# A loop over batches written out on all five engines of a fused attention and mixture-of-experts kernel

## Chip, core and metric

The kernel runs on one core of a Trainium2 chip. The metric is the device time of one launch in microseconds; lower is better. A core has five engines with an instruction stream each: TensorE (PE in the profile; its weight loads are PEld), VectorE (DVE), ScalarE (ACT), GpSimd (POOL) and SyncE (SP). They meet only at semaphores, and a transfer signals its end by a semaphore too. PEq, DVEq and so on in a row stand for the engine's sequencer, which reads the instructions, works out register values and takes the branches.

## What is computed

`x` is 4 batches x 1024 tokens x 256 features, `ctx` is 4 x 154 x 256. All data is float32.

```
x = x + softmax((LN(x) Wq + bq)(ctx Wk + bk)^T / 16, masked) (ctx Wv + bv)
t = LN(x)
scores = sigmoid(l2norm(t) l2norm(gate_w)^T)          # 16 experts
combine = the 8 largest scores of a token, divided by their sum, else 0
routed = sum over e of combine[e] * ((silu(t w_gate[e]) * (t w_up[e])) w_down[e])
shared = (silu(t sw_gate) * (t sw_up)) sw_down
x = x + routed + shared
```

## The kernel before

**Tiling.** The 4096 tokens are 8 chunks of 512 tokens, two chunks (`hf` 0 and 1) to a batch `b`. All 17 experts (the shared one is expert 0) are applied to every token; each expert's weights stay in SBUF, split into a high and a low part, so that every product is three matmuls (`three_pass`, L298 to L300). For one chunk and one expert PE does `gate_up`: twelve matmuls of 512 columns into `gate_ps` and `up_ps`, and `down`: twelve of 256 columns into `y_ps`. Between them ACT takes the tanh (`tanh_gate`, L666), DVE multiplies by gate and up (`silu_up`, L949 and L953), POOL multiplies by the combine weight (`weighted`, L1160), ACT copies out the high part (`hidden_hi`, L673) and DVE the low part (`hidden_lo`, L959). The hidden values have two buffers. `gate_up` runs three experts ahead of `down`.

**Order of work.** Each engine has a function `chunk(b, hf, ahead, last)` with one step for each of the 17 experts. In between the steps stand the parts of the *front* of the next chunk: layer norm, attention, second layer norm, router, put at steps written out by hand (`PE_AT`, `ACT_AT`, `DVE_AT`, `POOL_AT`). So PE's stream in a chunk is a fixed sequence: `down` 0, `gate_up` 3, `down` 1, `gate_up` 4 and so on, with the front's transposes (L386) and small matmuls between. The first transposes of the front (`turn_x`) come at step 2.5.

**Combine weights.** ACT stores the combine rows to memory (L659), and SP loads them again, two experts at a time, broadcast to all 128 partitions (`spread`, L256, 512 KB each written in SBUF) into four places `cb`. The first four of a chunk are issued together near the end of the chunk before. SP also loads the next `xin` (x rows) and stores the finished chunk (L272).

**The loop.** Before the loop each engine runs a prologue: keys, values, weight loads and splits, and the whole front of chunk 0. Then the chunks 0 to 5 stand in a hardware loop of three passes, one on each engine (SP L281, PE L555, ACT L750, DVE L1077, POOL L1191); chunks 6 and 7 are written out behind it:

```python
with pe.Fori(0, B - 1) as b:
    chunk(b, 0, True, False)
    chunk(b, 1, True, False)
chunk(B - 1, 0, True, False)
chunk(B - 1, 1, False, True)
```

Inside it `b` is a register, so every wait count that `upto` gives is worked out by the sequencer. `wait_apart` is used where such a count stands with other waits: it puts the counts in registers, waits for `consts_set` (long set), and then for the semaphores. A pass holds two chunks. A loop's branch stands on the loop's line in the profile; it is taken twice and falls through once.

Of the kernel before, what the change touches and what calls it, by code (L numbers as in the profile page):

```python
# [50 lines left out]
def xattn_moe_kernel(nc, x, ctx, mask, Wq, bq, Wk, bk, Wv, bv, gate_w, w_gate, w_up, w_down,  # L51
                     sw_gate, sw_up, sw_down, out):
    B, S, D = x.shape
    KEYS = ctx.shape[1]
    E, _, H = w_gate.shape
    TOK = 512
    TILES = TOK // P
# [21 lines left out]
    with ExitStack() as stack:  # L79
# [107 lines left out]
            return b * (2 * per) + (per * hf + k)  # L187

        def first_chunk(b, hf):
            return isinstance(b, int) and b == 0 and hf == 0  # L190

        def wait_apart(eng, *waits):


            counts = [n if isinstance(n, int) else eng.to_reg(n) for _, n in waits]
            eng.wait_ge(consts_set, 1)
            for (what, _), n in zip(waits, counts):
                eng.wait_ge(what, n)

        def due(table, step, at):  # L200
# [15 lines left out]
        def _(sp):  # L216
# [30 lines left out]
            def spread(b, hf, pair):  # L247

                stored_c = (c_stored, upto(b, hf, 16, 16))
                if pair >= PLACES:  # L250
                    wait_apart(sp, (h_done, upto(b, hf, NE, 2 * (pair - PLACES) + 3 + FREE)))
                elif first_chunk(b, hf):
                    wait_apart(sp, stored_c)
                else:
                    wait_apart(sp, (h_done, upto(b, hf - 1, NE, 2 * (pair + PLACES) + 3 + FREE)), stored_c)
                sp.dma_start(cb[:, pair % PLACES].rearrange("p a t -> p (a t)"),  # L256
                             c_rows[2 * pair:2 * pair + 2, :].rearrange("a t -> (a t)").partition_broadcast(P)) \
                    .then_inc(cb_loaded[pair % PLACES], 16)
# [4 lines left out]
            def chunk(b, hf, load):  # L263
                for pair in range(PLACES, PAIRS):
                    spread(b, hf, pair)
                if load:
                    sp.wait_ge(x2_made, upto(b, hf, 2, 4))
                    sp.dma_start(xin[:], x_rows[b * 2 + (hf + 2)]).then_inc(x_loaded, 16)
                for pair in range(PLACES):
                    spread(b, hf + 1, pair)  # L270
                sp.wait_ge(y_added, upto(b, hf, 2, 2 + FREE))
                sp.dma_start(out_rows[b * 2 + hf], x2[:, hf]).then_inc(stored, 16)  # L272
# [5 lines left out]
                    sp.dma_start(out_rows[CHUNKS - 1, :, 2 * q:2 * q + 2, :], x2[:, 1, 2 * q:2 * q + 2, :]) \  # L278
                        .then_inc(stored, 16)

            with sp.Fori(0, B - 1) as b:  # L281
                chunk(b, 0, True)
                chunk(b, 1, True)
            chunk(B - 1, 0, False)
# [7 lines left out]
        def _(pe):  # L292
# [96 lines left out]
            def turn_x(b, hf, k):  # L389
                if k == 0 and not first_chunk(b, hf):  # L390
                    pe.wait_ge(c_read, upto(b, hf, 1, 0))
                turn_ln(ln1_done, t1_turned, b, hf, k)
# [66 lines left out]
            def gate_up(b, hf, e):  # L459
                hf, e = nxt(hf, e)  # L460
                i, par = slot(hf, e), hf % 2
                if e == 0:
                    pe.wait_ge(t2_hi, upto(b, hf, 2, 2))
                    pe.wait_ge(t2_lo, upto(b, hf, 2, 2))
                if hf == 0:
                    pe.wait_ge(w_hi, e + 1)
                    pe.wait_ge(w_lo, e + 1)
                for ps, col, free, done in ((gate_ps, 0, silu_done, gate_done), (up_ps, UP0, prod_done, up_done)):
                    pe.wait_ge(free, upto(b, hf, NE, e - 1 + FREE))
                    ins = three_pass(ps[i][:], [((W[:, e, HI, col + k * H:col + (k + 1) * H],  # L470
                                                  W[:, e, LO, col + k * H:col + (k + 1) * H]),
                                                 (xT[:, par, HI, k, :], xT[:, par, LO, k, :])) for k in range(KD)],
                                     first=True, last=True)
                    ins.then_inc(done, 1)
# [38 lines left out]
            def chunk(b, hf, ahead, last):  # L513
                for s in range(NE):
                    down(b, hf, s)
                    if ahead:
                        front(s, b, hf + 1)
                    if s + 3 < NE or not last:
                        gate_up(b, hf, s + 3)
                    if ahead:  # L520
                        front(s + .5, b, hf + 1)
# [30 lines left out]
            turn_c(0, 0)  # L552
            gate_up(0, 0, 1)
            gate_up(0, 0, 2)
            with pe.Fori(0, B - 1) as b:  # L555
                chunk(b, 0, True, False)
                chunk(b, 1, True, False)
            chunk(B - 1, 0, True, False)
# [4 lines left out]
        def _(act):  # L563
# [47 lines left out]
            def split_w(e):  # L611
                act.wait_ge(staged[e % STAGES], 48 * (e // STAGES + 1))
                af(W[:, e, HI, :], stage[:, e % STAGES, :], ACT.Copy).then_inc(w_hi, 1)
# [36 lines left out]
            def combine_rows(b, hf):  # L650
                act.wait_ge(c_turned, upto(b, hf, 1, 1))
                if not first_chunk(b, hf):
                    act.wait_ge(c_stored, upto(b, hf, 16, 0))
                af(cT[0:E, :], f_ps[1][0:E, :], ACT.Copy).then_inc(c_read, 1)
                act.wait_ge(c_read, upto(b, hf, 1, 1))
                if not first_chunk(b, hf):
                    for done in cb_loaded:
                        act.wait_ge(done, upto(b, hf, 32, 0))
                act.dma_start(c_rows, cT[0:E, :]).then_inc(c_stored, 16)  # L659
# [32 lines left out]
            def chunk(b, hf, ahead, last):  # L692
                for s in range(NE):
                    if s + 2 < NE or not last:
                        tanh_gate(b, hf, s + 2)
                    if ahead:
                        front(s, b, hf + 1)
                    if s + 1 < NE or not last:
                        hidden_hi(b, hf, s + 1)
                    if ahead:  # L700
                        front(s + .5, b, hf + 1)
# [45 lines left out]
            hidden_hi(0, 0, 0)  # L747
            for e in SPLITS["end"]:
                split_w(e)
            with act.Fori(0, B - 1) as b:  # L750
                chunk(b, 0, True, False)
                chunk(b, 1, True, False)
            chunk(B - 1, 0, True, False)
# [4 lines left out]
        def _(dve):  # L758
# [57 lines left out]
            def split_w(e):  # L816
                dve.wait_ge(w_hi, e + 1)
                V_.tensor_tensor(W[:, e, LO, :], stage[:, e % STAGES, :], W[:, e, HI, :].bitcast(F32),
                                 ALU.subtract).then_inc(w_lo, 1)
# [184 lines left out]
            def chunk(b, hf, ahead, last):  # L1004
                for s in range(NE):
                    if s + 2 < NE or not last:
                        silu_up(b, hf, s + 2)
                    if ahead:
                        front(s, b, hf + 1)
                    if s + 1 < NE or not last:  # L1010
                        hidden_lo(b, hf, s + 1)
                    if ahead:
                        front(s + .5, b, hf + 1)
                add_y(b, hf)
# [59 lines left out]
            hidden_lo(0, 0, 0)  # L1074
            for e in SPLITS["end"]:
                split_w(e)
            with dve.Fori(0, B - 1) as b:  # L1077
                chunk(b, 0, True, False)
                chunk(b, 1, True, False)
            chunk(B - 1, 0, True, False)  # L1080
# [4 lines left out]
        def _(pool):  # L1085
# [61 lines left out]
            def weighted(b, hf, e):  # L1147
                hf, e = nxt(hf, e)
                i = slot(hf, e)
                if e == 0:  # L1150
                    wait_apart(pool, (prod_done, upto(b, hf, NE, 1 + FREE)), (h_hi, upto(b, hf, NE, FREE - 1)),
                               (h_lo, upto(b, hf, NE, FREE - 1)))
                    pg.tensor_scalar(h[:, i, :], ew[:, i, :], 0.5, 1.0, ALU.mult, ALU.mult).then_inc(h_done, 1)
                else:
                    pool.wait_ge(prod_done, upto(b, hf, NE, e + 1 + FREE))
                    pool.wait_ge(h_hi, upto(b, hf, NE, e - 1 + FREE))
                    pool.wait_ge(h_lo, upto(b, hf, NE, e - 1 + FREE))
                    pair = (e - 1) // 2
                    pool.wait_ge(cb_loaded[pair % PLACES], upto(b, hf, 32, 16 * (pair // PLACES + 1)))
                    pg.tensor_tensor(h[:, i, :], ew[:, i, :], cb[:, pair % PLACES, (e - 1) % 2, :], ALU.mult) \  # L1160
                        .then_inc(h_done, 1)
# [12 lines left out]
            def chunk(b, hf, ahead, last):  # L1174
                for s in range(NE):
                    if s + 1 < NE or not last:
                        weighted(b, hf, s + 1)
                    if ahead:
                        front(s + .5, b, hf + 1)
# [8 lines left out]
            ln2_std(0, 0)  # L1188
            inverse_norm(0, 0)
            weighted(0, 0, 0)  # L1190
            with pool.Fori(0, B - 1) as b:  # L1191
                chunk(b, 0, True, False)
                chunk(b, 1, True, False)
            chunk(B - 1, 0, True, False)
# [24 lines left out]
```

## Time and profile before

| | us |
|---|---|
| median of 3 runs | 715.76 |
| the runs | 711.46, 715.76, 718.47 |
| span of the profiled execution | 717.8 |
| PE busy in the span | 691.6 (96%) |
| PE weight loads busy | 595.8 (83%) |
| DVE busy | 459.2 (64%) |
| POOL busy | 260.7 (36%) |
| ACT busy | 239.8 (33%) |
| mean granted TensorE clock | 0.981 |

The profiled execution has no separately listed time beside its span of 717.8 us; that is the number the sums are made against. Busy time of PE is that of matmuls whose ends are modelled and which overlap, so 96% says that they followed one another closely, not that the array was used to its peak. A granted clock of 1.00 is 2.4 GHz, 0.50 is 1.2 GHz.

### The profile page before, as it was taken

The numbers are of one execution on the slowest core, as the hardware profiler recorded it, in microseconds if no ns is written. First come the engines' busy times: TensorE is split into PE (matmuls) and PEld (weight loads), VectorE is DVE, ScalarE is ACT, GpSimd is POOL, SyncE is SP. The second block draws the span as 40 slices with busy tenths as digits, with TensorE's granted clock in tenths as the row PEclk, the third lists the DMA queues.
The fourth block names the chain that finished last, engine by engine and source line by source line (L and its number), as shares of the span: only waits on it lengthen the run. The fifth ranks groups of instructions, "written<-read, shape, count | busy, mean of one in ns | idle before, by whom it ended". The sixth has DMA issues, their size and how long they took to land.

```text
span 717.8 us, 11775 instructions
## 1 busy us (share of the span) xinstructions
PE 691.6 (96%) x3995; PEld 595.8 (83%) x3995; DVE 459.2 (64%) x1029; ACT 239.8 (33%) x485; POOL 260.7 (36%) x222
## 2 busy tenths in 40 slices
PE   7997799999999899999999899999999999999997
PEld 6575688888888788888888788888988888888886
DVE  4576666677667475777566576677565775775444
ACT  4345233333424134233333234242334233232221
POOL 2120432535343242435344243434324343433432
PEclk9799999999999899999999999999999999999999
DMA  6315511032110510005100411005110421006100
GB/s 184 111 32 162 184 60 46 13 103 106 59 31 1 180 60 30 30 24 185 59 30 1 151 59 60 30 2 192 46 58 0 136 94 38 1 3 204 61 0 31
DMA packets 32772, 51.30 MB, mean 71 GB/s; under 512 B 3918, under 2 KB 24391, under 8 KB 32711
## 3 DMA queue, kind: packets, MB, share of 16 engines
q1 hardware_dynamic: 32455, 50.23, 21.6%
q8 instruction: 37, 0.61, 0.4%
q10 hardware_dynamic: 256, 0.26, 0.2%
q14 instruction: 24, 0.20, 0.1%
HBM read 46.03 MB, written 4.46 MB: 70 GB/s over the span
## 4 chain that ended last, share of the span: by engine, by line
PE 91%; issue 4%; DVE 2%; POOL 1%; ACT 1%; DMA 1%; POOLq 0%; SPq 0%; DVEq 0%; ACTq 0%
PE y_ps L298 9%; PE y_ps L300 9%; PE y_ps L299 9%; PE gate_ps L298 9%; PE up_ps L298 9%; PE gate_ps L300 9%; PE gate_ps L299 8%; PE up_ps L300 8%; PE up_ps L299 8%; PE f_ps L386 2%; PE f_ps L408 2%; PE f_ps L419 1%; PE up_ps L368 1%; PE up_ps L307 1%; DMA xin<-in_x_dram 1%
## 5 line engine op out<-in xcount | busy, mean ns | idle before, releaser
L1160 POOL TENSOR_TENSOR hidden<-hidden,cb 128x512 f32<-128x512 f32 x128 | 200.1, 1565 | 308.2 <-DVE hidden L953 257.4
L949 DVE SCALAR_TENSOR_TENSOR hidden<-hidden,gate_ps 128x512 f32<-128x512 f32 x136 | 93.2, 685 | 156.2 <-ACT hidden L666 145.9
L666 ACT ACTIVATE hidden<-gate_ps 128x512 f32<-128x512 f32 x136 | 81.5, 599 | 275.0 <-PE gate_ps L300 273.4
L298 PE MATMUL y_ps<-W,hs 128*128 128x256 f32 x544 | 157.9, 290 | 13.4 <-issue 5.7
L300 PE MATMUL y_ps<-W,hs 128*128 128x256 f32 x544 | 154.8, 284 | 0.0
L299 PE MATMUL y_ps<-W,hs 128*128 128x256 f32 x544 | 154.5, 284 | 0.0
L298 PEld LDWEIGHTS y_ps<-W,hs 128*128 128x128 f32 x544 | 103.8, 191 | 19.9 <-issue 9.5
L959 DVE TENSOR_TENSOR hs<-hidden,hs 128x512 fp32r<-128x512 f32 x136 | 95.6, 703 | 29.1 <-ACT hs L673 29.1
L298 PE MATMUL gate_ps<-xT,W 128*128 128x512 f32 x272 | 109.1, 401 | 0.0
L298 PE MATMUL up_ps<-xT,W 128*128 128x512 f32 x272 | 108.8, 400 | 0.0
L300 PE MATMUL gate_ps<-xT,W 128*128 128x512 f32 x272 | 108.2, 398 | 0.0
L299 PE MATMUL gate_ps<-xT,W 128*128 128x512 f32 x272 | 107.8, 396 | 0.0
L299 PE MATMUL up_ps<-xT,W 128*128 128x512 f32 x272 | 107.6, 396 | 0.0
L300 PE MATMUL up_ps<-xT,W 128*128 128x512 f32 x272 | 107.5, 395 | 0.0
L299 PEld LDWEIGHTS y_ps<-W,hs 128*128 128x128 f32 x544 | 103.9, 191 | 3.9
L953 DVE TENSOR_TENSOR hidden<-hidden,up_ps 128x512 f32<-128x512 f32 x136 | 93.6, 688 | 16.6 <-PE up_ps L300 1.9
L300 PEld LDWEIGHTS y_ps<-W,hs 128*128 128x128 f32 x544 | 103.9, 191 | 0.0
L673 ACT ACTIVATE hs<-hidden 128x512 fp32r<-128x512 f32 x136 | 85.2, 626 | 47.2 <-POOL hidden L1160 47.2
L300 PEld LDWEIGHTS up_ps<-xT,W 128*128 128x128 f32 x272 | 51.6, 190 | 12.8
L299 PEld LDWEIGHTS up_ps<-xT,W 128*128 128x128 f32 x272 | 52.0, 191 | 12.0
L298 PEld LDWEIGHTS up_ps<-xT,W 128*128 128x128 f32 x272 | 51.5, 189 | 12.1
L300 PEld LDWEIGHTS gate_ps<-xT,W 128*128 128x128 f32 x272 | 51.7, 190 | 11.6
(141 smaller groups left out, 726.3 us busy)
## 6 DMA issues: line engine op xcount, KB each, us to landing
cb<-c_rows SPq DMA_DIRECT2D x64, 512.0 KB, 4.2
xin<-in_x_dram SPq DMA_DIRECT2D x8, 512.0 KB, 3.8
out_dram<-x SPq DMA_DIRECT2D x7, 512.0 KB, 7.4
stage<-in_L_ffn_w_gate_dram SPq DMA_DIRECT2D x16, 128.0 KB, 2.3
stage<-in_L_ffn_w_up_dram SPq DMA_DIRECT2D x16, 128.0 KB, 2.5
stage<-in_L_ffn_w_down_dram SPq DMA_DIRECT2D x16, 128.0 KB, 2.6
cb<-in_ctx_dram SPq DMA_DIRECT2D x1, 512.0 KB
out_dram<-x SPq DMA_DIRECT2D x2, 256.0 KB, 2.1
```

Source lines behind the costliest of these rows:

```text
L298: mm(ps, lh, rh, start=first and i == 0, stop=False)
L299: mm(ps, lh, rl, start=False, stop=False)
L300: ins = mm(ps, ll, rh, start=False, stop=last and i == len(pairs) - 1)
L307: nc.tensor.transpose(up_ps[0][:, 0:P], ident[:], ident[:])
L386: ins = nc.tensor.transpose(f_ps[k][:, j * P:(j + 1) * P], xn[:, j, k * P:(k + 1) * P], ident[:])
L408: mm(to[:, 0:2 * KEYS], xT[:, par, HI, k, c], A[:, bi, k].rearrange("p s q -> p (s q)"), start=k == 0, stop=False)
L666: af(ew[:, i, :], gate_ps[i][:], ACT.Tanh, scale=0.5).then_inc(tanh_done, 1)
L673: af(hs[:, i, HI, :], h[:, i, :], ACT.Copy).then_inc(h_hi, 1)
L949: V_.scalar_tensor_tensor(out=ew[:, i, :], in0=ew[:, i, :], scalar=1.0, in1=gate_ps[i][:], op0=ALU.add, op1=ALU.mult).then_inc(silu_done, 1)
L953: V_.tensor_tensor(ew[:, i, :], ew[:, i, :], up_ps[i][:], ALU.mult).then_inc(prod_done, 1)
L959: V_.tensor_tensor(hs[:, i, LO, :], h[:, i, :], hs[:, i, HI, :].bitcast(F32), ALU.subtract) \
L1160: pg.tensor_tensor(h[:, i, :], ew[:, i, :], cb[:, pair % PLACES, (e - 1) % 2, :], ALU.mult) \
```

## The change

The five loops become Python loops, so that the program holds the body three times on each engine, with `b` a number: every wait count is a constant, and there is no loop register and no branch in the stream. `first_chunk` and `wait_apart` lose the parts that dealt with registers; `wait_apart` no longer waits for `consts_set`. Which engine does what, in which order, with which buffers and semaphores otherwise stays as it was.

```diff
         def first_chunk(b, hf):
-            return isinstance(b, int) and b == 0 and hf == 0
+            return b == 0 and hf == 0
 
         def wait_apart(eng, *waits):
-            counts = [n if isinstance(n, int) else eng.to_reg(n) for _, n in waits]
-            eng.wait_ge(consts_set, 1)
-            for (what, _), n in zip(waits, counts):
+            for what, n in waits:
                 eng.wait_ge(what, n)
...
-            with sp.Fori(0, B - 1) as b:
+            for b in range(B - 1):
                 chunk(b, 0, True)
                 chunk(b, 1, True)
             chunk(B - 1, 0, False)
...
-            with pe.Fori(0, B - 1) as b:
+            for b in range(B - 1):
                 chunk(b, 0, True, False)
                 chunk(b, 1, True, False)
             chunk(B - 1, 0, True, False)
```

The same edit as on PE is made on ACT, DVE and POOL.

## Rows read from the trace of the kernel before

**Rows 1.** The page: the span, and busy time of each engine with its share.

```profile
span 717.8 us, 11775 instructions
PE 691.6 (96%) x3995; PEld 595.8 (83%) x3995; DVE 459.2 (64%) x1029; ACT 239.8 (33%) x485; POOL 260.7 (36%) x222
```

**Rows 2.** The waits: engine, line, releaser: us in total, times, longest.

```profile
DVE hidden L949 <- issue: 9.9, 2, 5.0
PE y_ps L298 <- issue: 5.7, 2, 3.1
PE y_ps L298 <- ACT hs L673: 4.6, 1, 4.6
```

**Rows 3.** Windows: stretch, length, busy of PE, PEld, DVE, ACT, POOL, clock, DMA.

```profile
91.19:171.28 80.09, 80.09 (x478) 70.20 (x477) 54.52 (x124) 27.02 (x55) 31.87 (x26) 1.00 0.20 68
171.28:257.54 86.26, 83.17 (x478) 72.47 (x477) 54.07 (x124) 27.02 (x55) 31.63 (x26) 0.96 0.19 63
337.68:422.20 84.52, 81.90 (x478) 71.44 (x477) 54.03 (x124) 27.02 (x55) 31.65 (x26) 0.98 0.20 64
502.28:582.36 80.08, 80.08 (x479) 70.20 (x477) 54.56 (x124) 27.02 (x55) 31.88 (x26) 1.00 0.20 67
...
337.68:381.26 43.58, 43.58 (x266) 38.71 (x265) 27.72 (x62) 13.78 (x29) 17.39 (x15) 1.00 0.14 44
...
582.36:625.93 43.57, 43.57 (x266) 38.72 (x265) 27.74 (x62) 13.78 (x29) 17.44 (x15) 1.00 0.09 32
```

**Rows 4.** The loop lines' branches: duration ns min/median/max, first and last start us.

```profile
L555 PEldq COMPARE_BRANCH  x3: 76/5807/6276, 235.2 to 566.2; - x3
...
L1077 DVEq COMPARE_BRANCH  x3: 60/68/68, 236.1 to 567.1; - x3
...
L1191 POOLq COMPARE_BRANCH  x3: 40/45/45, 232.2 to 563.1; - x3
...
L750 ACTq COMPARE_BRANCH  x3: 40/45/50, 233.4 to 564.4; - x3
```

**Rows 5.** Timeline of PE around the three branches: start us, us, engine, line, what.

```profile
238.38 0.40 PE L300 MATMUL up_ps<-xT,W 128*128 128x512 f32 x1
241.87 0.58 PE L298 MATMUL y_ps<-W,hs 128*128 128x256 f32 x1 [3.09 <-issue]
...
407.76 0.38 PE L298 MATMUL y_ps<-W,hs 128*128 128x256 f32 x1 [2.62 <-issue]
...
569.34 0.40 PE L300 MATMUL up_ps<-xT,W 128*128 128x512 f32 x1
569.57 0.28 PE L298 MATMUL y_ps<-W,hs 128*128 128x256 f32 x1
```

**Rows 6.** Windows again: the stretch behind the first branch taken.

```profile
241.10:247.90 6.80, 6.03 (x20) 5.36 (x21) 1.98 (x3) 0.51 (x2) 2.84 (x2) 0.50 0.61 225
```

**Rows 7.** Timeline of DVE behind the first branch taken and behind the fall-through.

```profile
242.06 0.69 DVE L949 SCALAR_TENSOR_TENSOR hidden<-hidden,gate_ps 128x512 f32<-128x512 f32 x1 [4.92 <-issue]
...
569.00 0.69 DVE L949 SCALAR_TENSOR_TENSOR hidden<-hidden,gate_ps 128x512 f32<-128x512 f32 x1 [0.90 <-ACT hidden L666]
```

**Rows 8.** Timeline of POOL, DVE and PE in the chunk behind the fall-through.

```profile
569.59 2.54 POOL L1160 TENSOR_TENSOR hidden<-hidden,cb 128x512 f32<-128x512 f32 x2 [5.54 <-DMA cb<-c_rows]
...
571.58 1.11 DVE L959 TENSOR_TENSOR hs<-hidden,hs 128x512 fp32r<-128x512 f32 x1 [1.05 <-ACT hs L673]
...
573.77 0.28 PE L298 MATMUL y_ps<-W,hs 128*128 128x256 f32 x1
...
574.65 0.68 DVE L959 TENSOR_TENSOR hs<-hidden,hs 128x512 fp32r<-128x512 f32 x1
...
577.99 0.28 PE L298 MATMUL y_ps<-W,hs 128*128 128x256 f32 x1
```

**Rows 9.** The page's DMA queues: packets, MB, share of 16 engines.

```profile
q8 instruction: 37, 0.61, 0.4%
...
q14 instruction: 24, 0.20, 0.1%
```

More of the change, by code:

```diff
@@ L749, in _ @@
                 split_w(e)
-            with act.Fori(0, B - 1) as b:
+            for b in range(B - 1):
                 chunk(b, 0, True, False)
@@ L1076, in _ @@
                 split_w(e)
-            with dve.Fori(0, B - 1) as b:
+            for b in range(B - 1):
                 chunk(b, 0, True, False)
@@ L1190, in _ @@
             weighted(0, 0, 0)
-            with pool.Fori(0, B - 1) as b:
+            for b in range(B - 1):
                 chunk(b, 0, True, False)
```

## The prediction, made before the result was known

> **What bounds the kernel now.** I read the page first. PE is busy 691.6 us of a span of 717.8 [rows 1], so about 26 us of the span hold no matmul, and the question is which of them belong to the loop. The waits say who ended PE's idle time. Two gaps of 5.7 us together are "issue": the engine waited for nothing that the profile shows. DVE has two of the same kind, 9.9 us together. One gap of 4.6 us stands behind ACT's `hs` [rows 2]. It is the wait at expert 1 of chunk 0, where the combine rows arrive late behind the prologue's weight loads; no loop line takes part in it.
>
> Then I cut the span at the first transposes of each front (`turn_x`, L386, always step 2.5 of a chunk), so that each window is exactly one chunk of PE's fixed sequence and a chunk boundary lies inside it. The windows come in two kinds [rows 3]. Where the boundary is between the two halves of a pass, PE needs 80.09 us and is busy for all of it (four windows lie within 80.08 to 80.14; two of them stand in the rows). Where the boundary is the loop's return, it needs 86.26 and 84.52. The loop lines name the reason: PE's branch took 6.276 and 5.807 us the two times it was taken and 0.076 us when it fell through; the branches of DVE, ACT and POOL report 0.068 us at most [rows 4].
>
> The best witness is the window 502.28 to 582.36: it holds the third end of the body, the same last and first steps of a chunk, but PE falls through to new code, and the window takes 80.08 us. It is what the change makes of the other two boundaries. The reader is to see that the kernel is PE-bound in the steady state, with two holes at the returns.
>
> **The first return in detail.** PE's last matmul before it begins at 238.38 and its next at 241.87, after 3.09 us idle; at the second return the gap is 2.62; at the fall-through the starts are 569.34 and 569.57, no gap [rows 5]. The branch is read while matmuls are still queued, so only the part of its 6.3 us that outlasts them shows. The gap is not the whole price. From 241.10 to 247.90 the granted clock is 0.50, that is 1.2 GHz, after PE had stood idle from 238.78 [rows 5, 6]. The 6.03 us busy there would be about 3.0 at 2.4 GHz. So 3.09 idle and 3.0 lost to the clock make 6.1, and the windows say 86.26 - 80.09 = 6.17. DVE's hole of 4.92 us [rows 7] lies in the same time and is not added.
>
> **The change part by part.**
>
> *Returns of the loop, removed.* First: 86.26 - 80.09 = 6.17 us. Second: 84.52 - 80.08 = 4.44 us. Sum 10.61 us. All of it is on the path, since PE has no other gap in these windows. The differing figures have a reason: the idle parts are 3.09 and 2.62, the rest is how long the lower clock lasted.
>
> *The third pass's end and the entry.* The end costs nothing now (80.08 against 80.09), and nothing after. The entry into the loop is straight code before and after; its gaps are waits for data [rows 2]. Zero.
>
> *Register work, removed.* The first part of a chunk, `turn_x` to the second transposes, takes 43.58 us in the loop with register counts, and 43.57 in chunk 6 with constants [rows 3]. So this is worth 0.01 us a chunk: the sequencer does it while queued matmuls run. If that cover were gone, it would show as "issue" in these windows, and PE's busy time fills them. Zero. The missing `consts_set` wait in `wait_apart` never waits; what remains is one count waited for instead of two, and the same comparison of windows bounds it: zero.
>
> *Longer streams, added.* PE, DVE and SP read as many instructions as now. Whether ACT and POOL do is not plain: their branches take 0.050 us at most [rows 4] and no "issue" hole follows them, as if the body's start had still been there. Afterwards they must fetch three bodies instead of one. No row prices such a fetch when it isn't hidden except the two returns. From below it is zero: the fall-through window has ACT and POOL enter new code at no cost [rows 3]. From above, one costs DVE's hole of 4.92 us. I take zero, because rows of straight code are nearest: some 150 us of it at the end show no such gap on any engine, since PE's and DVE's two each in the waits are the two returns [rows 2].
>
> *What is late next.* With the hole gone, `down` of expert 1 could wait for its hidden values, since POOL is held up 5.54 us by the four `cb` loads issued together. At the fall-through these arrive in time: DVE finishes at 571.58 + 1.11 = 572.69, PE wants them at 573.77; 1.08 us to spare [rows 8]. SP's loads, issued at the same place of the chunk, are not moved past any other. Zero, but with the thinnest cover of the sum.
>
> **Sum.** 717.8 - 10.61 = 707.2 us against the profiled execution. That one is 2.0 us above the median of the runs, 715.76, about what one return differs from the other (1.73). Three ways to carry it over: if the median run paid the same, 705.2; from the fastest run, 711.46, taking off only the idle parts (3.09 + 2.62 = 5.71) as if its clock had never fallen, 705.8; from the slowest, 718.47, with two dear returns (12.3), 706.1. I forecast **706 us**.
>
> **A rule against the trace.** PE's branch takes 5.8 to 6.3 us when taken [rows 4]. The Trainium skill, Advanced Engine Details and Errata, section Control Flow Timing, gives about 51 ns for an unconditional and 108 ns for a compare-and-branch. By that figure the estimate for two returns is some 0.2 us, the time would stay at 715.5, and unrolling would be pointless. The measured number decides for PE; the rule describes the four branches of 0.04 to 0.07 us well, and DVE's then shows its 4.92 us only behind the branch.
>
> **The rivals.**
>
> *A. Half the holes stay (0.14).* The stream's own next piece may have to come just as the four `cb` loads of 512 KB take the transfer engines, and a hole of a return's size stays at one of the two boundaries. For it: the DMA share behind the return is 0.61 over 6.8 us [rows 6]. Against: the fall-through meets the same loads with no gap. Price: one return of 4.4 to 6.2 us stays, 706 + 5 = 711.
>
> *B. The holes are not the branch's (0.04).* The idle time would come back as a wait of another name: `cb` arriving later than 1.08 us of cover allows. For it: POOL's wait for `cb` is 5.54 us [rows 8]. Against: the fall-through. Price: no change, 715.
>
> *C. Slower: ACT or POOL starve for instructions (0.04).* ACT and POOL now read each body fresh. In the steady state the low part of `hs` is ready at 574.65 + 0.68 = 575.33 and PE wants it at 577.99 [rows 8], so 2.66 us of a fetch are covered; one as long as DVE's hole, 4.92, would cost PE 2.3 us, more with the clock. The queue that feeds the small streams carries about 8 KB a piece (0.20 MB in 24) and PE's 7990 matmuls and weight loads in 0.61 MB come to at most 76 B each [rows 1, 9], so a piece holds some 110. ACT's 485 and POOL's 222 instructions make 530 in six chunks, their waits perhaps as many: 8 to 10 pieces. Nine exposed ones cost 9 x 2.3 = 20.7 less 10.6: 716 + 10 = 726. It turns into a loss from five exposed pieces on. Against: prologue and chunks 6 and 7 are such code, and neither engine shows an "issue" gap.
>
> *D. More than forecast (0.03).* Returns in unprofiled runs are dearer than profiled ones: 701.
>
> **How the numbers follow.** Forecast 0.75, A 0.14, B 0.04, C 0.04, D 0.03. About 1% is what a measurement of this kernel can tell from no change; against 715.76 that is 708.6 and 722.9. The forecast's own spread comes from the runs before, 711.5 to 718.5, of which part is the returns' own; I give it 702 to 710, so nearly a tenth of it lies above 708.6. Faster by over 1%: 0.69 of the forecast's 0.75, some 0.03 of A, and D, 0.75. Slower: C, 0.04. Within 1%: the rest, 0.21. The range takes in A's 711 and the forecast's lower edge: 702 to 712.
>
> **What would show it.** Right: no COMPARE_BRANCH of microseconds in PE's stream; no "issue" wait at L298 and L949; all `turn_x` windows near 80.1 us; granted clock 1.00 from chunk 1 to chunk 6; PE's queue q8 at 37 pieces or a few fewer, and q14 at 24 or a few more. The span falls by 10.6 us. Wrong: windows at 84 to 86 with a gap before L298 (A, with `cb` as the releaser: B), or ACT and POOL waits named "issue" with PE waiting for `hs` behind them (C). If the windows are clean and the total is still above 710, the prologue or the tail has grown, which no step here foresees.

## The result

The changed kernel takes 706.12 us (median of 4 runs, 704.31 to 708.75) against 713.68 us of the kernel before (4 runs, 711.46 to 718.47); the ratio is 0.9883, 95% interval 0.9835 to 0.9931. Run again with more rounds beside the kernel before, it took 704.98 us (10 runs) against 714.27 (27 runs), ratio 0.9898, 0.9859 to 0.9936. So it is 1.0 to 1.2% faster, and the forecast of 706 is met within 0.2 us. Two of the profiles used below, the first one with one return and the one turned to step 1, are of the slowest run of their kernel. The profiled execution fell from 717.8 to 703.6 us.

The page of the kernel after, its span and the busy times, which answers to [rows 1]:

```profile
span 703.6 us, 10934 instructions
PE 685.5 (97%) x3995; PEld 592.4 (84%) x3995; DVE 461.6 (66%) x1029; ACT 239.8 (34%) x485; POOL 263.0 (37%) x222
```

The same compute instructions, 841 fewer in all: the register work and the branches. The windows from one `turn_x` to the next, columns as in [rows 3]:

```profile
87.55:167.66 80.11, 80.11 (x479) 70.22 (x477) 54.83 (x124) 27.01 (x55) 32.16 (x26) 1.00 0.20 67
167.66:247.78 80.12, 80.12 (x478) 70.20 (x477) 54.69 (x124) 27.00 (x55) 32.16 (x26) 1.00 0.21 67
...
327.90:407.98 80.08, 80.08 (x478) 70.19 (x477) 54.58 (x124) 27.01 (x55) 32.17 (x26) 1.00 0.18 66
...
488.07:568.14 80.07, 80.07 (x479) 70.18 (x477) 54.81 (x124) 27.00 (x55) 32.16 (x26) 1.00 0.20 67
```

The second and the fourth held 86.26 and 84.52 us before. They are now like the others, with PE busy all through and the granted clock at 1.00. DVE and PE around the first of these boundaries, which answers to [rows 5, 7, 8]; PE's first two lines stand where the return's gap was, the last two are the start of `down` of expert 1:

```profile
234.42 0.69 DVE L946 SCALAR_TENSOR_TENSOR hidden<-hidden,gate_ps 128x512 f32<-128x512 f32 x1 [0.90 <-ACT hidden L663]
...
236.68 1.18 DVE L956 TENSOR_TENSOR hs<-hidden,hs 128x512 fp32r<-128x512 f32 x1 [0.73 <-ACT hs L670]
```

```profile
234.76 0.40 PE L297 MATMUL up_ps<-xT,W 128*128 128x512 f32 x1
234.99 0.28 PE L295 MATMUL y_ps<-W,hs 128*128 128x256 f32 x1
...
238.96 0.40 PE L297 MATMUL up_ps<-xT,W 128*128 128x512 f32 x1
239.19 0.28 PE L295 MATMUL y_ps<-W,hs 128*128 128x256 f32 x1
```

DVE starts 0.90 us after its last work, as at the fall-through of before, not after 4.92. The low part of `hs` is ready at 236.68 + 1.18 = 237.86 and PE takes it at 239.19: the thin cover is there, 1.33 us of it. The instruction queues of the page, against [rows 9]:

```profile
q8 instruction: 32, 0.52, 0.3%
...
q14 instruction: 20, 0.16, 0.1%
```

Both became smaller. The loop had fetched more, not less: behind each return pieces were fetched anew.

**Where the span's 14.2 us are.** The two return windows give (86.26 - 80.12) + (84.52 - 80.08) = 10.6 us, the forecast's sum. The other 3.6 us are the time up to the first window, 91.19 against 87.55 us, in code that the change did not touch. Twelve profiles of kernels with that same prologue, these two among them, put this moment at 84.8 to 96.3 us; section 7 below shows what goes with it. So these 3.6 us lie within the scatter between executions.

### The profile page after: what moved, and what is told of

Read it like the earlier page. It is cut to its first block, busy times and chain, and to the rows that moved or that the text cites. A ratio compares the mean times of both kernels' runs of the same rounds, so it can differ in the third digit from the quotient of the medians.

```text
span 703.6 us, 10934 instructions
## 1 busy us (share of the span) xinstructions
PE 685.5 (97%) x3995; PEld 592.4 (84%) x3995; DVE 461.6 (66%) x1029; ACT 239.8 (34%) x485; POOL 263.0 (37%) x222
## 4 chain that ended last, share of the span: by engine, by line
PE 89%; DVE 3%; DMA 2%; ACT 2%; issue 1%; SPq 1%; POOL 0%; POOLq 0%; DVEq 0%
PE y_ps L295 9%; PE y_ps L297 9%; PE y_ps L296 9%; PE gate_ps L295 9%; PE up_ps L295 9%; PE gate_ps L297 9%; PE gate_ps L296 9%; PE up_ps L297 9%; PE up_ps L296 9%; PE f_ps L383 2%; PE f_ps L405 1%; PE f_ps L416 1%; DMA cb<-c_rows 1%; DMA xin<-in_x_dram 1%; PE up_ps L304 1%
## 5 line engine op out<-in xcount | busy, mean ns | idle before, releaser
L956 DVE TENSOR_TENSOR hs<-hidden,hs 128x512 fp32r<-128x512 f32 x136 | 97.9, 719 | 27.3 <-ACT hs L670 27.3
```

The source lines that it names most:

```text
L956: V_.tensor_tensor(hs[:, i, LO, :], h[:, i, :], hs[:, i, HI, :].bitcast(F32), ALU.subtract) \
```

## The experiments

### 1. Which engine's loop pays: PE alone, DVE alone, both, the other three

Each kernel is the one before, with the loops of some engines written out (`with pe.Fori(0, B - 1) as b:` becomes `for b in range(B - 1):`) and register counts kept elsewhere.

PE alone:

> Only PE's loop is written out; SP, ACT, DVE and POOL keep theirs. Theory T (the price is the refetch of instructions behind a taken branch, on PE itself): PE's own hole of 3.09 and 2.62 us goes. DVE still stands 4.9 us behind each of its two taken branches; at the fall-through of the kernel before it began its next silu_up at 569.00 where with the hole it begins at the equivalent of 573.0, finishes the low part of hs for expert 1 at about 575.1, and PE wants that at 573.8. So PE waits about 1.3 us twice, now behind DVE or ACT and not 'issue'; the chunk windows from turn_x to turn_x with a return in them are 81.4 to 83 us (the clock may fall or not), the clean ones 80.1; time 3 to 6 us above the fully written-out kernel, about 709 to 711. Rival (a return's price is paid as long as any engine jumps, by the meeting at semaphores): windows stay 84.5 to 86.3 and the time stays at the kernel before's, about 714. Rival (only PE's jump matters): 80.1 in all windows, 706.

DVE alone:

> Only DVE's loop is written out. Theory T: PE still has its branch of 5.8 to 6.3 us at two returns, its last queued matmuls cover some 3.4 us of it, so windows with a return stay 84.5 to 86.3 us with 'issue' before y_ps; DVE's 'issue' hole of 4.9 us is gone but nobody was waiting for it. Time as the kernel before, about 714, ratio 1.00 within 0.4%. Rival (DVE's hole is the one that sets the end): windows 80.1 and 706.

PE and DVE:

> PE's and DVE's loops are written out; SP, ACT and POOL keep theirs, with register counts. Theory T: all six windows 80.1 us, no 'issue' wait at y_ps or silu_up, time equal to the kernel that is written out everywhere, about 706 (704 to 709). Rival (part of the gain comes from ACT, POOL or SP, or from the register counts there): windows or time stand between, 708 to 712.

SP, ACT and POOL:

> SP's, ACT's and POOL's loops are written out; PE and DVE keep theirs. Theory T: as the kernel before, windows with a return 84.5 to 86.3, time about 714, ratio 1.00 within 0.4%. Rival (those three bring part of the gain): 708 to 711. It also tests whether ACT and POOL starve when they read each body fresh: then a clean window would be over 80.2 us.

| written out | us (runs) | ratio, 95% | windows with a return |
|---|---|---|---|
| PE | 715.06 (10) | 0.9974, 0.9928 to 1.0020 | 83.71, 83.89 |
| DVE | 717.53 (10) | 1.0047, 0.9990 to 1.0105 | 84.88, 84.38 |
| PE, DVE | 707.84 (4) | 0.9878, 0.9775 to 0.9981 | 80.12, 80.09 |
| SP, ACT, POOL | 716.35 (10) | 1.0039, 0.9984 to 1.0094 | 84.89, 85.53 |

The kernel before took 716.36 us beside them (25 runs). By the windows PE and DVE together give the whole gain, and the other three give none, register counts included. The times of PE alone (709 to 711 expected) and of DVE alone (714 expected) came out higher; the runs of DVE alone lie 11 us apart.

With DVE alone written out PE's branches still take 5.89 and 6.13 us, and its gaps of 2.95 and 2.71 us stand at the same place. The profile now names DVE's and ACT's `hs` for them and not "issue", as was expected; the length of the branches says that the name is not the cause. The windows with PE and DVE written out:

```profile
176.42:256.54 80.12, 80.12 (x478) 70.20 (x477) 54.70 (x124) 27.02 (x55) 31.97 (x26) 1.00 0.20 67
336.66:416.75 80.09, 80.09 (x478) 70.20 (x477) 54.55 (x124) 27.01 (x55) 31.94 (x26) 1.00 0.20 67
```

With SP, ACT and POOL alone the clean window between the two returns stays at 80.12 us, so neither ACT nor POOL starves on straight code in this profile:

```profile
251.97:332.09 80.12, 80.12 (x478) 70.21 (x477) 54.52 (x124) 27.01 (x55) 31.96 (x26) 1.00 0.21 68
```

PE alone is the instructive one. The rows are DVE's start behind its branch, then PE's two waits and the first window; the releaser of PE's waits in brackets is now DVE's `hs`:

```profile
242.51 0.69 DVE L949 SCALAR_TENSOR_TENSOR hidden<-hidden,gate_ps 128x512 f32<-128x512 f32 x1 [5.47 <-ACT hidden L666]
...
243.83 0.68 DVE L959 TENSOR_TENSOR hs<-hidden,hs 128x512 fp32r<-128x512 f32 x1
```

```profile
244.66 0.36 PE L298 MATMUL y_ps<-W,hs 128*128 128x256 f32 x1 [1.79 <-DVE hs L959]
...
408.67 0.36 PE L298 MATMUL y_ps<-W,hs 128*128 128x256 f32 x1 [2.01 <-DVE hs L959]
...
171.17:254.88 83.71, 81.92 (x479) 71.35 (x477) 54.58 (x124) 27.11 (x55) 31.67 (x26) 0.98 0.19 64
```

The hole of PE is gone and a second one, hidden beneath it, comes to light. I had expected 1.3 us and windows up to 83; it is 1.8 to 2.0, and behind it the granted clock falls (0.98 over the window), which brings it to 83.71 - 80.12 = 3.6 us. DVE stood 5.47 us here and not 4.9. By these windows (86.26 - 83.71 and 84.52 - 83.89) PE's loop is worth about 3.2 of 10.6 us alone, DVE's 1.5 alone, both together everything. One profile each can't tell 1.5 us from nothing: with SP, ACT and POOL alone the same two windows differ from those of the kernel before by 1.4 us down and 1.0 up. What is clear is that prices of overlapping holes can't be added, nor tested one at a time.

### 2. One return instead of two

```diff
+            chunk(0, 0, True, False)
+            chunk(0, 1, True, False)
-            with pe.Fori(0, B - 1) as b:
+            with pe.Fori(1, B - 1) as b:
                 chunk(b, 0, True, False)
                 chunk(b, 1, True, False)
```

The same on all five engines. It was run twice.

> The first pass of all five loops is written out ahead of the loop, which then has two passes: one return instead of two. Theory T (a price for each taken branch): window 171 to 257 is 80.1 us, the one at 408 to 492 is 84.4 to 86.3; time half way, 708 to 711. Rival (a loop costs by being there, by its entry or its register counts): both windows as in the kernel before.

> One return again. In its first profile the one return that was left cost 8.4 us (window 88.5) and not 4.4 to 6.2: PE waited twice, 1.57 us for its own refetch and 3.64 us for DVE, which stood 6.4 us behind its branch and 2.1 us more a few instructions later, as if its next piece had come late too. Theory (the price hangs on where the target lies in a fetched piece): again two gaps and a window of 87 to 89; and the entry window at 254 to 335 back to 80.1, where it was 81.1 for a late store of the combine rows. Rival (an accident of a disturbed run): window 84.4 to 86.3, time half way, 709 to 711.

The first time it took 714.51 us against 715.39 (ratio 0.9982, 0.9938 to 1.0026), the second time 711.12 against 714.27 (0.9970, 0.9939 to 1.0001). Neither is resolved from no change as a time, and both lie above what was expected. The windows of the second profile are clear; of what was expected of it, the theory's two gaps came true, but with the rival's window, 84.40 us. Windows without and with the return, then PE's waits, then DVE's:

```profile
255.30:335.42 80.12, 80.12 (x478) 70.20 (x477) 54.55 (x124) 27.00 (x55) 31.87 (x26) 1.00 0.20 68
335.42:419.82 84.40, 80.62 (x478) 70.04 (x477) 54.83 (x124) 27.11 (x55) 31.43 (x26) 1.00 0.20 65
```

```profile
403.80 0.38 PE L300 MATMUL y_ps<-W,hs 128*128 128x256 f32 x1 [0.92 <-issue]
411.17 0.36 PE L300 MATMUL y_ps<-W,hs 128*128 128x256 f32 x1 [2.86 <-DVE hs L965]
```

```profile
406.21 0.69 DVE L955 SCALAR_TENSOR_TENSOR hidden<-hidden,gate_ps 128x512 f32<-128x512 f32 x1 [4.97 <-issue]
409.56 1.46 DVE L965 TENSOR_TENSOR hs<-hidden,hs 128x512 fp32r<-128x512 f32 x1 [1.94 <-issue]
```

The boundary that is straight now costs nothing, the one with a return 84.40 - 80.12 = 4.3 us. So the price goes by the return and not by there being a loop. Its make-up is another than in the kernel before: PE's own hole is 0.92 us, and DVE stops twice, 4.97 us behind the branch and 1.94 us two instructions on. That second stop, with no wait that the profile shows, was there in both profiles of this kernel and not in the kernel before. The transfers bear on it. q14 brings pieces of instructions to the small streams, and a narrow window of the DMA view shows when a piece starts. One starts at 404.27 and DVE goes on 1.94 us later; the next starts at 407.72 and DVE goes on 1.84 us later. In the kernel before, the same distance is 1.93 us (240.13 to 242.06), and with PE alone written out 1.94. So both stops fit a wait for a piece. That the second is there because DVE's target lies near the end of the first piece is the likeliest reading; the runs do not show the pieces' borders, so this is argued. In the first profile the same return cost 8.4 us, with PE's gaps at 1.57 and 3.64 us, the pieces later (404.94 and 408.54) and the granted clock at 0.96 over the window, where the second profile has 1.00; why the two differ is open.

### 3. Why a return takes so long: the loads beside it

Three kernels keep all loops. One turns PE's and DVE's bodies, so that their returns come at step 13 of an even chunk, where hardly a transfer runs:

```diff
-            with pe.Fori(0, B - 1) as b:
-                chunk(b, 0, True, False)
+            chunk(0, 0, True, False, range(0, TURN))
+            with pe.Fori(0, B - 1) as b:
+                chunk(b, 0, True, False, range(TURN, NE))
                 chunk(b, 1, True, False)
-            chunk(B - 1, 0, True, False)
+                chunk(b + 1, 0, True, False, range(0, TURN))
+            chunk(B - 1, 0, True, False, range(TURN, NE))
```

> All loops kept; PE's and DVE's bodies are turned, so that their return stands at step 13 of an even chunk and not at its start. Around step 13 (546 to 564 us in the kernel before) hardly any transfer is under way, while behind the old return the transfer engines are at a share of 0.6 to 1.0. Theory T1 (the refetch is slow because it queues behind the four cb loads): PE's branch takes about 2 us instead of 5.8 to 6.3, is covered by the queued matmuls, no hole; all windows 80.1 to 80.5, time 706 to 708. Theory T2 (a refetch takes 4 us or more wherever it is): PE's branch still takes over 5 us, a gap of 2 to 3 us before a matmul in each turned window, time as the kernel before, 712 to 715. Instruction counts are nearly those of the kernel before, so a gain here also says that it is not the register work.

A control turns them by one step only, `TURN = 1`, which leaves the return among the loads:

> As the kernel turned to step 13, but the return stands at step 1 of an even chunk, where the cb loads and the store of the finished chunk are still under way (share 1.0 from 486 to 496 us). T1: branch of PE 4 to 6 us and holes of 1 to 3 us, time 710 to 715. T2: the same as at step 13. So this and the one before differ only by what the transfer engines do at the return.

The third leaves the returns in place and takes away the loads instead, but for an eighth:

```diff
                 for pair in range(PLACES):
-                    spread(b, hf + 1, pair)
+                    spread(b, hf + 1, pair, 16 if hf else P)
```

> The kernel before with all its loops; the four cb loads issued just ahead of each return go to 16 partitions instead of 128 (an eighth of the bytes; the other partitions keep old combine weights, so the results of those chunks are not the reference's). The returns stay where they were. T1 (the refetch queues behind those loads): PE's branch falls to about 3.5 us as in the body turned to step 13, its gap to under 1 us, windows with a return 80.1 to 81.5, and the time to 705 to 709. T2 (it is the place in the program, not the loads): branch 5.8 us or more and windows 84 and over, time as before. The store of the finished chunk, issued 3 us behind the loads, is kept.

| kernel | PE's branches, us | windows with a return | us (runs) | ratio, 95% |
|---|---|---|---|---|
| before | 6.28, 5.81 | 86.26, 84.52 | | |
| turned to step 13 | 3.54, 3.61 | 80.80, 80.84 | 707.65 (4) | 0.9876, 0.9804 to 0.9947 |
| turned to step 1 | 6.73, 6.69 | 86.51, 85.18 | 716.62 (10) | 0.9986, 0.9942 to 1.0030 |
| returns in place, small loads | 3.56, 3.45 | 80.80, 80.61 | 706.21 (10) | 0.9908, 0.9874 to 0.9943 |

The clean windows of the body turned to step 1 are 80.07 to 80.12 us at a granted clock of 1.00, as in the other kernels. The last kernel leaves old combine weights in 112 of 128 partitions; it is there for its time alone.

The windows of exactly the first branch's duration (the last three numbers are the granted clock, the share of the transfer engines and GB/s), for the body turned to 13, the one turned to 1, and the small loads:

```profile
291.28:294.82 3.54, 3.35 (x15) 2.05 (x13) 1.73 (x4) 0.75 (x2) 1.68 (x1) 1.00 0.03 7
```

```profile
239.99:246.72 6.73, 3.54 (x19) 2.67 (x17) 2.20 (x3) 1.75 (x3) 3.17 (x3) 0.95 0.83 273
```

```profile
231.70:235.26 3.56, 3.56 (x19) 2.67 (x17) 1.92 (x4) 1.12 (x2) 1.29 (x1) 1.00 0.37 132
```

In all three PE has 3.35 to 3.56 us of matmuls in the branch's window. A branch of 3.5 us is nearly covered by them: PE is idle for 0.46 us behind the first at step 13, and for 0.38 and 0.26 with the small loads. One of 6.7 leaves a hole, and after it the clock falls. Moving the return away from the loads and moving the loads away from the return do the same thing. The theory T1 holds, with two corrections: I expected about 2 us in the quiet place and it is 3.5, so 0.7 us a return remains (80.80 against 80.12); and the branches of the body turned to step 1 take 6.7 us, not 4 to 6.

Whether the fetch waits or merely runs more slowly can be read from the transfers. In each of these windows exactly one piece of PE's instruction queue q8 starts, of 0.02 MB. Here it is in the kernel before (window 239.10 to 239.60) and in the body turned to step 13 (292.28 to 292.78):

```profile
q8 instruction: 1, 0.02, 11.6%
```

```profile
q8 instruction: 1, 0.02, 14.3%
```

The share is one of 16 engines over 0.5 us, so the piece itself took 0.93 us among the loads and 1.14 us without any: the loads do not lengthen it. What they lengthen is the time until it starts:

| return | branch, us | piece starts after, us | from there to the branch's end, us |
|---|---|---|---|
| before, first | 6.28 | 3.91 | 2.37 |
| before, second | 5.81 | 3.50 | 2.31 |
| turned to step 1, first | 6.73 | 4.37 | 2.36 |
| one return, second profile | 4.10 | 1.63 | 2.47 |
| turned to step 13, first | 3.54 | 1.03 | 2.51 |
| small loads, first | 3.56 | 1.04 | 2.52 |

So the part from the piece's start on is 2.3 to 2.5 us everywhere, and what the loads add stands ahead of it: 1.0 us in the quiet place, 1.6 to 4.4 among them. How much it is the share alone doesn't tell; with one return it was 1.63 us at a share of 0.88. The Trainium skill, Runtime: NRT & Kernel Launch, section Instruction fetch mechanics, says that a taken branch whose target is outside the window must first fetch its page by DMA; the trace agrees, one piece of q8 and 3.5 us with the transfer engines idle, and adds that the piece starts later among the kernel's own loads, which makes 4.1 to 6.7 us.

### 4. What bounds the start: an earlier load

PE's largest idle stretch in the changed kernel is at expert 1 of chunk 0, 3.27 us. SP issues the first `cb` load there behind the weights of experts 15 and 16. On top of the changed kernel:

```diff
             for e in range(NE):
+                if e == NE - 2:
+                    spread(0, 0, 0)
                 if e >= STAGES:
...
-            for pair in range(PLACES):
+            for pair in range(1, PLACES):
                 spread(0, 0, pair)
```

> The written-out kernel, and in SP's prologue the first cb load (experts 1 and 2) is issued ahead of the weight loads of experts 15 and 16 instead of behind them. PE's last idle stretches, 2.1 and 3.3 us at the start of chunk 0, stand behind POOL's wait for this load. Theory (that load's place in SP's queue sets chunk 0's start): the wait at expert 1 of 3.3 us goes, perhaps part of the low clock behind it; 2 to 6 us less than the written-out kernel, 700 to 704. Rival (the weight loads, pushed back, hold ACT in its order before the hidden values): no change or up to 2 us more.

It took 701.92 us (4 runs, 701.03 to 704.44), ratio to the kernel before 0.9795, 0.9721 to 0.9869, the lowest median seen. The changed kernel took 704.98 on the same chip (section 5), so the load's place is worth about 3 us, with overlapping ranges. POOL's wait for the load falls from 13.29 us to 7.59, and PE's at expert 1 from 3.27 to 0.46; first POOL and PE of the changed kernel, then of this one:

```profile
73.17 2.49 POOL L1157 TENSOR_TENSOR hidden<-hidden,cb 128x512 f32<-128x512 f32 x2 [13.29 <-DMA cb<-c_rows]
...
76.36 0.55 PE L295 MATMUL y_ps<-W,hs 128*128 128x256 f32 x1 [3.27 <-ACT hs L670]
```

```profile
69.19 1.28 POOL L1159 TENSOR_TENSOR hidden<-hidden,cb 128x512 f32<-128x512 f32 x1 [7.59 <-DMA cb<-c_rows]
...
75.28 0.36 PE L297 MATMUL y_ps<-W,hs 128*128 128x256 f32 x1 [0.46 <-DVE hs L958]
```

### 5. The changed kernel again

> The changed kernel again, with more rounds, beside the kernel before on the same chip: six windows of 80.1 us; ratio 0.985 to 0.989, since the two returns cost 10.6 us in one profile and 10 in others, and the prologue's clock adds some us either way.

Six windows of 80.08 to 80.12 us, ratio 0.9898 (0.9859 to 0.9936). The expectation said 0.985 to 0.989; the interval overlaps that, the value lies just outside.

### 6. The spread of the runs

In the prologue PE idles 1.1 to 1.5 us at about 25 us. Twelve transposes of the identity were put there, on top of the earlier load:

```diff
             pe.wait_ge(brow_scaled, 2)
+            for _ in range(12):
+                nc.tensor.transpose(f_ps[0][:, 0:P], ident[:], ident[:])
             pe.wait_ge(a_lo, 4)
```

> The written-out kernel with the early cb load, and twelve more transposes of the identity on PE in the prologue ahead of the first scores, where PE otherwise idles 1.1 to 1.5 us at about 25 us; in profiles so far the granted clock then fell to 0.50 for 3 to 20 us in most runs and not at all in others. Theory (this idle stretch throws the coin that spreads the runs by several us): no low clock between 25 and 46 us, runs within 3 us of each other, median 698 to 701. Rival (the spread is from earlier gaps, at 7 and 13 us, or from elsewhere): same median as the early cb load alone, 702, and the same spread.

702.63 us (5 runs, 701.24 to 703.51), ratio 0.9848, 0.9822 to 0.9875. The median missed the theory's 698 to 701; it is the rival's. From 25 to 46 us the granted clock was 1.00, but so it was in both profiles of the changed kernel, without the transposes. The spread is small, 2.3 us, but the kernel with the earlier load alone spread by 3.4 us in 4 runs; whether the transposes do anything isn't shown.

### 7. What the profiles say of the prologue

No kernel was made for this; the windows from 0 to the first `turn_x` of two profiles whose code is alike up to there, first with PE and DVE written out, then the changed kernel again, and from 25 to 46 us of the same two:

```profile
0.00:96.33 96.33, 80.58 (x365) 59.70 (x366) 57.14 (x142) 38.03 (x77) 20.83 (x31) 0.84 0.42 127
...
25.00:46.00 21.00, 20.48 (x65) 12.98 (x66) 8.19 (x27) 8.05 (x22) 0.80 (x2) 0.51 0.14 43
```

```profile
0.00:86.30 86.30, 70.97 (x365) 54.16 (x366) 57.19 (x142) 37.69 (x77) 20.82 (x31) 0.94 0.47 142
...
25.00:46.00 21.00, 19.30 (x119) 13.65 (x120) 14.39 (x46) 10.52 (x29) 3.60 (x8) 1.00 0.19 58
```

In 21 us the one gets 65 matmuls done at a granted clock of 0.51, the other 119 at 1.00. The kernel before had 0.76 there, the changed one 1.00. This is 10 us between two executions of the same work, as much as the whole effect of the change, and it decides how well a run's time can tell the two kernels apart. The two were taken on different chips, but that does not explain it: on the second one's chip the two profiles with one return had 0.59 there and reached their first `turn_x` at 93.4 and 95.1 us. Why the clock takes the one course or the other is open.

## Why the prediction was right

**The returns' price, 10.61 us.** Right: 10.6 us less in the same two windows of the profiled pair. Reading the fall-through as the model of the changed boundary was what made it exact, and experiments 1 to 3 confirm that it is the taken branch, waiting for its piece, and not the loop. The price is no constant: the return left in experiment 2 cost 8.4 us in one profile and 4.3 in the other.

**Idle plus clock.** Right as a split: 1.00 in all windows now. In experiment 2 a return of 4.3 us came without a fall of the clock (0.92 + 2.86 idle), so the clock's part is not in every return.

**DVE's hole lies in the same time and is not added.** Right for the sum, and more than I said: left alone it costs PE 1.8 to 2.0 us and with the clock 3.6 to 3.8 a return (experiment 1). The prediction gave what was late next as `cb`; had only PE been straightened, it would have been DVE.

**Register work zero.** Right: with PE's and DVE's counts constant and the other three engines' in registers the windows are 80.12 and 80.09; in the kernel before, with registers everywhere, the clean ones are the same.

**Longer streams zero, rival C.** The time was right, and so was the premise that ACT and POOL would need more pieces: with SP, ACT and POOL alone written out q14 rises from 24 to 28. What I left out is that DVE's pieces come by the same queue, and that it fetches fewer without returns and register instructions: with DVE alone written out q14 falls to 18. So it ended at 20, not at 24 or a few more. Nothing starved.

**Rival A, half the holes stay.** Did not happen: both boundaries have the four loads at the same place, and no gap. My argument against it was weaker than it looked, since at the fall-through no piece of q8 starts between 562 and 576 us, so it did not test PE's stream. The changed kernel does: at its second boundary a piece starts between 398.25 and 398.50 us, where the share of the transfer engines is 1.03, and that window takes 80.08 us. The rival's physics was true all the same for fetches behind a branch: they start later among these loads (experiment 3). That straight code is spared because it asks for its next piece early is the likely reason, but the traces show when a piece starts and not when it was asked for.

**The rule on branch times.** The 0.1 us of the Trainium skill (Advanced Engine Details and Errata, Control Flow Timing) would have left the time unchanged. For PE's taken branch it is off by a factor of 33 in a quiet place (3.5 us) and 62 in a busy one (6.7); PE's branches that fall through, 0.076 to 0.083 us, lie a little under it. The prediction says that it describes the four short branches well; those of DVE, ACT and POOL, 0.04 to 0.07 us, are about half of it.

**From the profile to the median.** Here lay the forecast's looseness, and that it is met within 0.2 us is luck: the runs of the changed kernel lie 4.4 us apart. The difference is 7.6 us by the first medians and 9.3 by the second, under the 9.8 that I had from 715.76; a fourth run of before, 711.61, brought that median down to 713.68. Both the prologue's clock and the returns' price vary between executions, and which of them made the earlier runs high is not known. The size of the effect is best taken from the windows of profiles: the two returns cost 10.6 us in one and 10.2 in another (84.89 and 85.53).

## What to carry to other kernels

Read a loop's return by cutting the trace at a fixed instruction of the body: windows with a return against those without give its price, and a last pass that falls through shows what straight code would do. The branch is cheap only as long as the engine's queued work outlasts the fetch of its target, here 3.5 us in a quiet place and up to 6.7 among loads; so write the loop out, or, where the program must stay small, put the return where no bulk transfer runs and much work is queued: that alone brought all but 0.7 us a return. Straighten all engines that fetch anew together, as the holes of two lie over one another, and look at the prologue's clock before believing a difference of single runs.

## What was not expected

- Behind a branch DVE's sequencer reports 0.068 us and yet DVE then stands idle for 3.8 to 6.4 us (1.8 to 2.4 with few transfers beside it), while PE's reports the whole 3.5 to 6.7 us itself. The duration of a branch isn't a price; the gap behind it is.
- A taken branch of PE takes 3.5 us with the transfer engines at a share of 0.03 and 6.7 at 0.83, where the four loads of 512 KB are under way. The piece itself takes about 1 us in both; it starts 1.0 us behind the branch in the one and 4.4 in the other.
- The same prologue runs at a granted clock of 0.51 or 1.00 for 21 us, from one execution to another, and ends 10 us apart.
